# Swapping the DMA queues of three stores (attention output, residual x1, quantized q8) in a one-layer transformer kernel

## The reference

```python
x = x + _layernorm(_L0_attn_ref(_layernorm(x), Wq, bq, Wk, bk, Wv, bv, Wo, bo))
x = x + _layernorm(_L0_ffn_ref(_layernorm(x), weight, w_scale, bias))

# attention: q, k, v = x Wq + bq, x Wk + bk, x Wv + bv per head
probs = softmax(q k^T * D**-0.5 + causal)
return (probs v, heads joined) @ Wo + bo

# ffn
scale = max(absmax(x, row), 1e-7) / 127
q = clip(round(x / scale), -128, 127)           # int8
out = (q @ weight^T) * scale * w_scale + bias
```

## Time and profile before

| what | us |
|---|---|
| two runs timed | 3951.72 and 4033.84 (median 3992.78) |
| the profiled execution, its own time | 3955.34 |
| its span on the slowest core (core 1) | 3953.8 |
| spans of the 8 cores | 3938.1 to 3953.8 |
| TensorE / DVE / ACT / GpSimd busy in the span | 2606.4 / 1103.4 / 1095.3 / 151.9 |
| stage C1, about | 3007 to 3420 of the span |

### The profile page before, as it was taken

One profiled execution on the slowest core, in us unless ns is written; L12 is line 12 of the kernel. 1 busy time (PEld: TensorE's weight loads), 2 busy tenths in 40 slices (PEclk: granted clock), 3 DMA queues, 4 the chain that ended last, 5 costly groups with the idle time before them and its releaser, 6 DMA issues.

```text
span 3953.8 us, 33766 instructions; the slowest of 8 cores (3938.1 to 3953.8 us)
## 1 busy us (share of the span) xinstructions
PE 2606.4 (66%) x11368; PEld 1137.4 (29%) x11368; DVE 1103.4 (28%) x1897; ACT 1095.3 (28%) x1714; POOL 151.9 (4%) x44
## 2 busy tenths in 40 slices
PE   0000019999787789887789877788875899135644
PEld 0000004444333334333334333334332333012221
DVE  0006201111033322333322333222332666302212
ACT  0003200000044334544334454335451222101111
POOL 0000000000000000000000000000000000013323
PEclk9999999999888889888889888899886877567777
DMA  9998880000200111000111000111005344443233
GB/s 126 136 171 299 214 157 38 38 38 38 69 17 17 27 27 27 24 13 18 27 27 27 21 14 21 27 27 27 6 1 181 128 131 135 122 75 102 79 85 96
DMA packets 351212, 282.26 MB, mean 71 GB/s; under 512 B 321090, under 2 KB 321090, under 8 KB 337474
## 3 DMA queue, kind: packets, MB, share of 16 engines
q1 hardware_dynamic: 202564, 162.64, 14.1%
q0 software_dynamic: 3072, 41.94, 7.9%
q10 hardware_dynamic: 145408, 75.52, 7.2%
HBM read 191.92 MB, written 117.44 MB: 78 GB/s over the span
## 4 chain that ended last, share of the span: by engine, by line
PE 49%; DVE 13%; ACT 10%; ACTq 8%; another core or an unknown queue 7%; issue 4%; DMA 4%; POOL 3%; SPq 1%; DVEq 1%; POOLq 0%
PE ps_b L362 11%; PE ps_v L264 11%; PE ps_b L380 7%; PE ps_b L523 6%; PE ps_b L528 6%; PE ps_b L481 6%; ACTq L803 4%; DVE bn6b L638 3%; ACT P_sb L492 3%; DVE t L410 2%; DMA xln_h<-xlnb 2%; ACTq L220 2%; ACT kT L370 2%; POOL att L845 2%
## 5 line engine op out<-in xcount | busy, mean ns | idle before, releaser
L492 ACT ACTIVATE P_sb<-ps_b,negb 128x512 bf16<-128x512 f32 (+3 forms) x1280 | 686.5, 641 | 107.1 <-PE ps_b L481 105.4
L523 PE MATMUL ps_b<-P_sb,v_sb 128*128 128x512 bf16 (+3 forms) x1280 | 458.9, 359 | 64.5 <-DVE P_sb L500 50.7
L264 PE MATMUL ps_v<-wv_all,xT 128*128 128x512 bf16 x2048 | 443.9, 380 | 46.5 <-DMA wv_all<-wv_r 46.5
L362 PE MATMUL ps_b<-xT,wkh 128*128 128x512 bf16 x2048 | 446.8, 380 | 22.9 <-DMA wkh<-wk_bf 22.8
L528 PE MATMUL ps_b<-P_sb,ones_sq 128*128 128x512 bf16 (+3 forms) x1280 | 453.7, 359 | 0.0
L824 PE MATMUL ps_c<-big,qTj 128*128 128x512 bf16 x1024 | 239.5, 399 | 306.7 <-DMA qTj<-q_h 306.7
L481 PE MATMUL ps_b<-qT,kT 128*128 128x512 bf16 (+3 forms) x1280 | 429.5, 364 | 6.6 <-DVE negb L456 6.6
L236 PE MATMUL ps_v<-bv_sb,ones_f 1*128 1x512 f32 x8 | 7.2, 1072 | 528.8 <-DMA xT<-xln_h 528.8
L380 PE MATMUL ps_b<-xT,wqh 128*128 128x512 bf16 x1024 | 259.5, 421 | 81.0 <-ACT kT L370 81.0
L264 PEld LDWEIGHTS ps_v<-wv_all,xT 128*128 128x128 bf16 x2048 | 200.7, 98 | 290.8 <-issue 50.4
L362 PEld LDWEIGHTS ps_b<-xT,wkh 128*128 128x128 bf16 x2048 | 199.9, 98 | 263.1 <-issue 26.5
(11 more groups left out here) (75 smaller groups left out, 1688.7 us busy)
## 6 DMA issues: line engine op xcount, KB each, us to landing
xin<-x_seq SPq DMA_DIRECT2D x48, 1024.0 KB, 8.1
xln_h<-xlnb ACTq DMA_DIRECT2D x32, 512.0 KB, 8.1
v_nat<-vout SPq DMA_DIRECT2D x32, 512.0 KB, 2.6
v_sb<-v_nat SPq DMA_DIRECT2D x512, 32.0 KB, 1.9
x_h<-x1b ACTq DMA_DIRECT2D x16, 1024.0 KB, 8.2
x1c<-x_h SPq DMA_DIRECT2D x16, 1024.0 KB, 8.1
out<-att SPq DMA_DIRECT2D x16, 1024.0 KB, 4.7
wq_bf<-wq_r POOLq DMA_DIRECT2D x1, 8192.0 KB, 88.2
```

The source lines that it names most:

```text
L264: tmm = P.do("tensor", lambda t, par=par, kc=kc, ncc=ncc, st=st: t.matmul(ps_v[:, par * 4 + ncc, :], xT[:, kc, st * 128:(st + 1) * 128], w ...
L362: tmm = P.do("tensor", lambda t, par=par, kc=kc, nc8=nc8: t.matmul(ps_b[:, nc8, :], wkh[:, par, kc, :], xT[:, kc, nc8 * 512:(nc8 + 1) * 51 ...
L492: t_e = P.do("scalar", lambda sc, i2=i2, qoff=qoff: sc.activation(P_sb[:, i2, qoff:512], ps_b[:, i2, qoff:512], AF.Exp, bias=negb[:, :], s ...
L523: P.do("tensor", lambda t, par=par, kt=kt, qcp=qcp, qoff=qoff, first=first, is_last=is_last, i2=i2: t.matmul(ps_b[:, 4 + qcp, qoff:512], v ...
```

## The change

Three stores change the engine that issues them. The attention output store (L562) goes from SP to ACT. The x1 store (L728) and the q8 store (L767) of C1 go from ACT to SP. Data, sizes, semaphores, the waits of each store and the place of each call in the code stay as they are.

```diff
@@ attention, end of head h
-                    t_ytst[h] = P.do("sync", lambda s, h=h: s.dma_start(
+                    t_ytst[h] = P.do("scalar", lambda s, h=h: s.dma_start(
                         out=yt_hb[h, :, :], in_=yT_sb[:, :]),
                         after=[t for t in t_yev], sem="yt", n=16)
@@ c1_tail(j)
-                t_x1st[j] = P.do("scalar", lambda s, j=j, jp=jp: s.dma_start(
+                t_x1st[j] = P.do("sync", lambda s, j=j, jp=jp: s.dma_start(
                     out=x1_h[j * 128:(j + 1) * 128, :], in_=x1b[:, jp, :]),
                     after=[t_x1[j]], sem="x1s%d" % jp, n=16)
@@ c1_tail(j)
-                t_q8st[j] = P.do("scalar", lambda s, j=j, jp=jp: s.dma_start(
+                t_q8st[j] = P.do("sync", lambda s, j=j, jp=jp: s.dma_start(
                     out=q8_h[j * 128:(j + 1) * 128, :], in_=qnat[:, jp, :]),
                     after=[t_qn], sem="q8%d" % jp, n=16)
```

## The result

The changed kernel is slower by 1.04%: ratio of times 1.0104, 95% interval 1.0089 to 1.012, from 8 timed runs of the changed kernel (3989.37 to 3995.44 us; their median lies near 3992) against 3 of the kernel before (3946.80 to 3953.49). On 3951 us, that is 41 us. The forecast sum was 38 us and 3993 us.

A forecast was written before the change was run, and what follows sets the result against it. The serial DVE and ACT tail was taken to pace C1 at 24.16 us a tile. Seven loops, each 5.5 us too long, add 38 us to 3955.3: 3993 us, range 3950 to 4050.

The forecast's parts named there:

- The sum: Whole kernel: seven late even tiles in C1 add 38 us to the profiled 3955.3, giving 3993 us.
- The bound: C1: serial work of DVE and ACT sets 24.16 us a tile; TensorE is ready 17.4 us early.
- Where the loads stood before: C1 on SP: yTj loads of tile j were issued mid-tail of tile j-2, now at that tail's end.
- Attention, taken as 0: Attention store L562 on ACT: issued over 23 us before ACT is wanted; 0 us, bounded by -5 and +5.
- What leaves ACT, taken as 0: C1: two issues a tile, 0.34 and 0.36 us, fall in ACT's idle gaps; gain 0, at most 11 us.
- The loop: C1, q8 store of tile j-2 to that of tile j: 53.8 us against 48.3 for two tiles, 5.5 too long.
- How often: C1: the 5.5 us is paid by tiles 2, 4, ..., 14, seven times, 38 us; odd tiles add nothing.
- Rival A: C1: loads as slow behind the q8 store as behind xin2; slower by over 2%, 90 us, 4045; chance 13%.
- Rival B: C1: TensorE stays fast; 3955 at 17.55 us a tile, 3972 at 20.9, so not slower; chance 19%.
- Rival C: C1: ACT's freed issues count and loads are early enough; 11 us less, 3944, or no effect; chance 6%.

The follow-up runs named there:

- the last kernel: Next tile's four bn_stats listed ahead of the conversion L757 on DVE, plus all three moved stores, against the kernel before: ratio 1.0368, 145 us slower.

## Where the prediction was right, and which step failed

**The step that failed** is the one that placed the result. The prediction gave its sum as 3993 us beside a median of before of 3992.8 and said that "a change under 2% (79 us) is about what a measurement of this kernel cannot tell from none". Read against that median the forecast says no change. That median was the mean of two runs of which one was 2% above the other, and no level to stand beside. The measured level before is 3947 to 3953 us, and the change was told clearly from none: 41 us slower, 1.04%, with an interval of 0.15% to each side. The sum itself said a slowdown of 1%, and that should have been the stated direction. The mechanism and the size held, as the rest of this section shows term by term.

- **The bound.** "TensorE is ready 17.4 us before it is needed": these reserves were what the change spent. With the x1 store alone on SP a part of them went (17.4 to 10.2 us in the tile shown), without any cost; with the q8 store they were overdrawn.
- **Where the loads stood before** was misread by one tile. The prediction says that the loads of tile j were issued "in the middle of that tail", the tail of tile j-2. The loads at 3187.36 go out in the tail of tile 6 and are for tile 9, which TensorE began at 3208.62; the matmuls of tile 7, for which they waited, had ended at 3184.27. So they went out in the tail of tile j-3, and the change moves them back by a tile and a half, some 39 us, not by 15. The sum starts at the q8 store and does not use this, so it came out right all the same.
- **Attention, taken as 0.** The kernel with that store alone shows it, 1.0001.
- **What leaves ACT, taken as 0.** No kernel moved a C1 store off ACT to anywhere but SP, but the x1 store alone was worth nothing (1.0001), so its 16 issues gained nothing.
- **The loop.** Forecast 53.8 us, measured 53.98 on average and 54.57 in the one above. The terms were off in both directions: the loads from first issue to TensorE's start 5.61 us, where I had 4.2 + 0.7 + 0.05 = 4.95; the tail 24.68 in that loop instead of 24.32; TensorE's tile 23.74 instead of 23.97. No run separates the 0.7 us taken for the q8 store's bytes ahead of the loads from the loads themselves; only the 5.61 for both is measured.
- **How often.** "Paid by tiles 2, 4, ..., 14" and "tile 3 adds nothing of its own": the profile has exactly seven waits. The two kernels with extra matmuls add what I had only half seen: the odd tiles run a loop of their own behind the even one and come out as soon as that gets shorter.
- **The sum.** 38 us forecast; 39.0 in C1 of core 1, 41 by the ratio.
- **Rival A** (loads as slow as in rows 8) did not come: TensorE started 5.6 us after the first issue, not 12.2. **Rival B** (TensorE fast) named the right lever. Without the bias matmuls the cost is zero. But its premise, that TensorE would be fast, was wrong: after 6.8 to 10.8 us of idle time, more than the 5 us that the prediction expected, each even tile had its bias at 7.16 us. **Rival C** fell with the two kernels at 1.0001.

On the rule of the Trainium skill that I weighed (TensorE: Matmul & The Clock Gate, "HAM oscillation — how this bites in real kernels"), that a loop which waits for a DMA before every tile starts each tile at the low clock: this case's trace agrees for the even tiles: the bias took 7.16 us after each wait of 6.8 us and more, and in the loop shown the granted clock over these matmuls (3112.09 to 3119.20) was 0.50, the lower of the two levels. After waits of 0.4 to 2.2 us before odd tiles the bias took 4.7 to 6.1 us.

## What to carry to other kernels

A `dma_start` is an instruction in an in-order list. Before a store is put on another queue, look at which loads stand behind it there, and add up the loop that this closes: store, loads, the work that needs the loads, and the work up to the next store; it costs only what the loop exceeds the present pace, and nothing while a reserve covers it. Put loads that run ahead in front of a store that ends a tile, or keep the two on different engines. And an edit that puts a wait for the next tile ahead of the store can turn a 1% order mistake into 4%, as the last kernel shows.

## What was not expected

- Work given to an idle TensorE shortened C1 (402 to 387 us with 20 extra matmuls a tile), though it stands ahead of the tile that everything waits for. Yet of the seven tiles without a wait on core 1 only one had the full clock and the time of the earlier trace rows; the six others had 0.91 and 19.3 us. Why the clock stays below full in them was not tried.
- With the x1 store alone on SP, TensorE waited 14 times for its loads, 36.5 us in all, and the kernel lost nothing. A column of waits in a profile is not a cost until the engine that sets the pace shows one.
